# Contracting the gate broadcasts and logit turns of a two-layer PLE kernel over all 128 partitions

## Chip, cores and metric

The kernel runs on one core of one Trainium2 chip. The metric is the device time of one launch in microseconds (us). A core has TensorE (PE; its weight loads, PEld, are recorded apart), VectorE (DVE), ScalarE (ACT), GpSimd (POOL) and the queue engine SyncE (SP). Each engine works through its own instructions in order; semaphores tie them together.

## What is computed

For 1024 samples five table rows of 1024 numbers are gathered, and two layers of gated experts and a small tower run on them. A layer (T = 4 tasks, E = 10 experts, two of them shared) is:

```python
eo = relu(einsum('bed,edh->beh', xe, W) + b)
gates = softmax(einsum('btd,tdk->btk', x[:, :T, :], Gw) + Gb, axis=-1)
task_out = einsum('btk,btkh->bth', gates, sel_eo)      # k = 4: two own experts, two shared
gs = softmax(x[:, T, :] @ Gsw + Gsb, axis=-1)          # layer 0 only, over all 10 experts
shared_out = einsum('be,beh->bh', gs, eo)
```

The task outputs of layer 1, joined with 16 dense features, go through relu(4112 x 512), relu(512 x 256) and 256 x 1.

## The kernel before

The batch is worked in two halves of N = 512 samples. Activations lie transposed, features on the 128 partitions and samples on the 512 columns, so that everything the experts compute is a matmul with a 128 x 128 weight tile held in the array and 128 x 512 activations moving. Every fp32 product is made of three fp32r products (high x high, high x low, low x high) in the helper `three` (L296 to L298). One unit (`unit`, L300) is 8 x 3 such matmuls, the output of one 128-row strip of an expert, and a step is 16 units, two experts.

SP loads a raw weight tile for each unit, ACT rounds it (L498, w_hi), DVE subtracts (L797, w_lo), and PE multiplies. ACT takes each result out of PSUM with bias and relu (L502); DVE multiplies experts by gates and adds (L866, L872). The next step's activations are split by ACT (L513) and DVE (L804).

Gates are made alongside, within the first four units of each gated step (`gated_step`, L382). There are 18 gated steps: in each half one for the shared gates of layer 0, four for its tasks, and four for the tasks of layer 1. The order on PE is written out by hand through `between`, which puts instructions after the three matmuls of tile k of a unit:

- unit 0: `logits` (L331, L333), two matmuls per tile k, with a 128 x 66 gate-weight tile held in the array, into bank gps[0]. ACT copies the result into `logit_t` (L529), rows 0 to 7 or 0 to 19; row 32 holds ones and meets the bias row of `comb`.
- unit 1, after k = 3: `turn_logits` (L339, L351). Four fp32 matmuls with 33 rows: 33 x 128 of `logit_t` is held, `comb` (33 x 4 or 33 x 10) moves. This adds the high and low parts and the bias, and turns the logits so that samples lie on partitions. DVE and ACT make the softmax out of them (L818).
- unit 2, after k = 1: `turn_gates` (L362, L365), four matmuls that turn the gates back. ACT copies 12 rows into `gate_t`, which lies over the first 12 partitions of the gate-weight tile `gw` (L97, L538).
- unit 2, after k = 4, 6, 7, and unit 3, after k = 1, 3: `broadcast` (L369, L378). One matmul per gate, with 12 rows: a column of `pick`, repeated 128 times, is held, `gate_t` (12 x 512) moves, and the gate comes out on all 128 partitions. ACT copies it to `gate_b` (L521), which DVE reads. A shared step makes 2 broadcasts (both after k = 4), a task of layer 0 makes 6 (two after k = 4, the rest one by one), a task of layer 1 makes 4 (two after k = 4, one after k = 6, one in unit 3).

From the third broadcast on, PE waits before each (L376) until ACT has emptied the bank that it writes. Between layers the 16 dense features are multiplied with 16-row matmuls (L474). The input rows are gathered by POOL (L287) and turned by DVE (L939) during the first step of each half.

Before the loops DVE clears tiles and makes `pick` (L1023 to L1043), and ACT starts the loads of the constants, those of `comb` among them (L683 to L687).

Of the kernel before, what the change touches and what calls it, by code (L numbers as in the profile page):

```python
# [31 lines left out]
B, D, T, NE = 1024, 1024, 4, 10  # L32
P = 128
HALVES, N = 2, 512
# [7 lines left out]
NG = T  # L42
LOGIT_ROWS = 66
ONES_ROW = 32
# [19 lines left out]
def build(nc, ids, dense_t, tbl_0, tbl_1, tbl_2, tbl_3, tbl_4, w0, w1, w_top, w_dense, w_top2, w_top3,  # L64
          b0, b1, b_top1, b_top2, gs_w, g_w, g_b, comb_s, comb_t, gs_b, ident_in, out):
    f32, f32r, i32 = mybir.dt.float32, mybir.dt.float32r, mybir.dt.int32
    ALU, ACT, AX = mybir.AluOpType, mybir.ActivationFunctionType, mybir.AxisListType
# [3 lines left out]
    with ctx:  # L71
        def sb(name, shape, dt=f32):
            return ctx.enter_context(nc.sbuf_tensor(name, shape, dt))

        def bank(name):
            return ctx.enter_context(nc.psum_tensor(name, [P, N], f32))

        def sem(name):
            return ctx.enter_context(nc.semaphore(name))
# [12 lines left out]
        prod = sb("prod", [P, 2, N])  # L92
        gw_raw = sb("gw_raw", [P, KT * NE])
        gw = sb("gw", [P, KT, LOGIT_ROWS], f32r)
        logit_t = sb("logit_t", [ONES_ROW + 1, N])

        gate_t = gw[0:12, :, :].rearrange("p k n -> p (k n)")[:, 0:N]  # L97
        comb = sb("comb", [ONES_ROW + 1, NE + NG])
        comb_sh, comb_tk = comb[:, 0:NE], comb[:, NE:]
        lg = sb("lg", [P, NBT, NE])  # L100
        small = sb("small", [P, 2 * NBT + 2])
# [1 line left out]
        gsh = sb("gsh", [P, NBT, NE])  # L103
        g6 = sb("g6", [P, NBT, 6])
        g12 = sb("g12", [P, NBT, LOGIT_ROWS], f32r)
        pick = sb("pick", [12, 6], f32r)
        ident = prod[:, 0, 0:P]
        ident_r = sb("ident_r", [P, P], f32r)
        idx = sb("idx", [P, IDX], i32)
# [6 lines left out]
        gps = [bank(f"gps{i}") for i in range(2)]  # L116
# [35 lines left out]
        bc_done = sem("bc_done")  # L152
        gb_rdy = sem("gb_rdy")
        chain = sem("chain")
# [3 lines left out]
        y_done = sem("y_done")  # L158
        y_rdy = sem("y_rdy")
        pre_rdy = sem("pre_rdy")  # L160

        block = ctx.enter_context(nc.Block())

# [129 lines left out]
        def _(pe):  # L293
# [75 lines left out]
            def broadcast(Q, R, order, places):  # L369

                def emit(k):
                    for n in [i for i, at in enumerate(places) if at == k]:
                        if n == 0:
                            pe.wait_ge(gt_evac, Q + 1)
                        if n >= 2:
                            pe.wait_ge(gb_rdy, R + n - 1)  # L376
                        j = order[n]
                        nc.tensor.matmul(gps[1 - n % 2][:, :], pick[:, j:j + 1].broadcast_to([12, P]),  # L378
                                         gate_t, start=True, stop=True).then_inc(bc_done, 1)
                return emit  # L380

            def gated_step(U, E, S, Q, R, order, shared=0):  # L382
# [63 lines left out]
            for h in range(HALVES):  # L446
# [37 lines left out]
                n = T - 2  # L484
# [9 lines left out]
        def _(act):  # L494
# [187 lines left out]

            for dst, src in ((bias0, b0), (bias1, b1), (bias_t1, b_top1), (bias_t2, b_top2), (w3, w_top3)):  # L683
                act.dma_start(dst[:, :], src).then_inc(consts_in, 16)
            act.dma_start(comb_sh[0:ONES_ROW, :], comb_s).then_inc(consts_in, 16)
            act.dma_start(comb_sh[ONES_ROW:ONES_ROW + 1, :], gs_b).then_inc(consts_in, 16)
            act.dma_start(comb_tk[0:ONES_ROW, :], comb_t).then_inc(consts_in, 16)  # L687
# [89 lines left out]
        def _(dve):  # L777
            class Count:

                start, n = 0, 0  # L780

            links = Count()

            def link(ins):

                links.n += 1
                ins.then_inc(chain, 1)
                return links.start + links.n

            def after(value):  # L790
                dve.wait_ge(chain, value)
# [233 lines left out]
            nc.vector.memset(g6[:, :, :], 0.0).then_inc(chain, 1)  # L1025
            nc.vector.memset(warm[:, :], 0.0).then_inc(chain, 1)
            nc.vector.memset(g12[:, :, :].bitcast(f32), 0.0).then_inc(chain, 1)
            links.n = 5
            after(5)
            dve.wait_ge(idx_in, 16)  # L1030
            for q in range(Q4):
                part = idx[q * 32:(q + 1) * 32, NBT:]
# [6 lines left out]
            put_in_order(0)  # L1039
            dve.wait_ge(ident_rdy, 16)  # L1040

            after(link(nc.vector.tensor_tensor(pick[:, :], prod[0:12, 0, 0:6], prod[0:12, 0, 6:12], ALU.add)))
            nc.vector.tensor_copy(ident_r[:, :], ident).then_inc(pre_rdy, 1)  # L1043
            dve.wait_ge(pre_rdy, 1)
            put_in_order(2)
# [155 lines left out]
```

## Time and profile before

| | |
|---|---|
| median of 3 runs | 2163.16 us (2161.07 to 2168.05) |
| span of the profiled execution, first to last instruction | 2130.1 us |
| what lies around the span, by subtraction from the median | 33.1 us |
| PE busy | 98% |
| DVE busy | 64% |
| ACT busy | 36% |
| POOL busy | 7% |
| mean granted TensorE clock | 0.996 |

In the rows below a timeline row is: start, duration, engine, line, operation, output<-inputs, shape, count, and in brackets the idle time before it with what ended it. A matmul `12*128 12x512` has 12 rows and 128 columns held in the array, and 12 x 512 moving. Matmuls are pipelined, so their durations overlap; the distance from start to start says what one costs. A row with x8 stands for eight instructions in succession, and its second number reaches from the first's start to the last's end.

### The profile page before, as it was taken

The numbers are of one execution on the slowest core, as the hardware profiler recorded it, in microseconds if no ns is written. First come the engines' busy times: TensorE is split into PE (matmuls) and PEld (weight loads), VectorE is DVE, ScalarE is ACT, GpSimd is POOL, SyncE is SP. The second block draws the span as 40 slices with busy tenths as digits, with TensorE's granted clock in tenths as the row PEclk, the third lists the DMA queues.
The fourth block names the chain that finished last, engine by engine and source line by source line (L and its number), as shares of the span: only waits on it lengthen the run. The fifth ranks groups of instructions, "written<-read, shape, count | busy, mean of one in ns | idle before, by whom it ended". The sixth has DMA issues, their size and how long they took to land.

```text
span 2130.1 us, 27384 instructions
## 1 busy us (share of the span) xinstructions
PE 2096.8 (98%) x9148; PEld 1678.2 (79%) x9148; DVE 1361.7 (64%) x1521; ACT 774.0 (36%) x1068; POOL 151.4 (7%) x152
## 2 busy tenths in 40 slices
PE   7999999999999999999998999999999999999999
PEld 6878787778878787878786787877887787878787
DVE  4668787886256665646656687877853466556564
ACT  3243333333333333332433333334333333433333
POOL 5700000000000000000455000000000000000000
PEclk9999999999999999999999999999999999999999
DMA  6623223222233222223454222232332222323231
GB/s 193 189 88 98 80 89 89 89 89 89 81 91 97 87 94 87 89 89 99 137 162 148 81 95 80 88 90 87 90 98 81 89 89 89 99 79 97 82 97 40
DMA packets 62801, 208.08 MB, mean 98 GB/s; under 512 B 11668, under 2 KB 11988, under 8 KB 62742
## 3 DMA queue, kind: packets, MB, share of 16 engines
q1 hardware_dynamic: 54432, 186.30, 28.6%
q0 software_dynamic: 7488, 20.98, 3.1%
q8 instruction: 27, 0.44, 0.1%
q14 instruction: 32, 0.26, 0.0%
q10 hardware_dynamic: 822, 0.09, 0.0%
HBM read 207.34 MB, written 0.00 MB: 97 GB/s over the span
## 4 chain that ended last, share of the span: by engine, by line
PE 89%; POOL 6%; issue 2%; DVE 2%; ACT 1%; DMA 1%; POOLq 0%; ACTq 0%; DVEq 0%
PE main L296 26%; PE main L298 25%; PE main L297 25%; POOL eo_b L287 6%; PE top L296 3%; PE top L298 3%; PE top L297 3%; PE gps L331 2%; PE gps L333 2%; PE gps L378 1%; PE gps L351 1%; DVE act_lo L804 1%; DVE slots L939 0%; DMA eo_sh<-in_tbl,idx 0%; DVE w_lo L797 0%
## 5 line engine op out<-in xcount | busy, mean ns | idle before, releaser
L296 PE MATMUL main<-act_hi,w_hi 128*128 128x512 f32 x2568 | 1012.9, 394 | 13.9 <-DVE act_lo L804 8.4
L298 PE MATMUL main<-act_hi,w_lo 128*128 128x512 f32 x2568 | 1002.1, 390 | 0.0
L297 PE MATMUL main<-act_lo,w_hi 128*128 128x512 f32 x2568 | 1001.6, 390 | 0.0
L797 DVE TENSOR_TENSOR w_lo<-raw,w_hi 128x1024 fp32r<-128x1024 f32 (+1 forms) x360 | 439.5, 1221 | 675.2 <-ACT w_hi L498 674.6
L498 ACT ACTIVATE w_hi<-raw 128x1024 fp32r<-128x1024 f32 (+1 forms) x360 | 380.4, 1057 | 1064.7 <-PE main L298 959.5
L296 PEld LDWEIGHTS main<-act_hi,w_hi 128*128 128x128 f32 x2568 | 482.8, 188 | 143.0 <-issue 30.9
L298 PEld LDWEIGHTS main<-act_hi,w_lo 128*128 128x128 f32 x2568 | 482.9, 188 | 101.9
L297 PEld LDWEIGHTS main<-act_lo,w_hi 128*128 128x128 f32 x2568 | 483.2, 188 | 97.5
L872 DVE TENSOR_TENSOR slots<-slots,prod 128x1024 f32<-128x1024 f32 (+1 forms) x200 | 244.7, 1223 | 5.9
L287 POOL DMA_INDIRECT eo_b<-in_tbl,idx x144 | 147.3, 1023 | 1001.2 <-DVE slots L872 915.9
L866 DVE TENSOR_TENSOR prod<-eo_sh,gate_b 128x1024 f32<-128x1024 f32 x136 | 165.6, 1218 | 1.0
L804 DVE TENSOR_TENSOR act_lo<-slots,act_hi 128x512 fp32r<-128x512 f32 x216 | 132.6, 685 | 4.1 <-ACT act_hi L631 2.5
L513 ACT ACTIVATE act_hi<-slots 128x512 fp32r (+1 forms) x208 | 119.1, 624 | 15.2 <-DVE slots L939 9.3
L296 PE MATMUL top<-act_hi,w_hi 128*128 128x512 f32 x264 | 103.3, 391 | 4.5 <-DVE act_lo L1010 4.5
L298 PE MATMUL top<-act_hi,w_lo 128*128 128x512 f32 x264 | 103.4, 392 | 0.0
L297 PE MATMUL top<-act_lo,w_hi 128*128 128x512 f32 x264 | 103.4, 392 | 0.0
L502 ACT ACTIVATE eo_b<-main,bias 128x512 f32<-128x512 f32 x128 | 85.8, 671 | 3.0 <-DVE slots L872 1.7
L502 ACT ACTIVATE slots<-main,bias 128x512 f32 (+1 forms) x128 | 85.5, 668 | 0.0
L872 DVE TENSOR_TENSOR slots<-slots,eo_b 128x1024 f32 (+1 forms) x64 | 78.3, 1223 | 2.5
L866 DVE TENSOR_TENSOR slots<-slots,gate_b 128x1024 f32 (+1 forms) x64 | 78.0, 1218 | 0.0
L866 DVE TENSOR_TENSOR eo_b<-eo_b,gate_b 128x1024 f32<-128x1024 f32 x64 | 78.0, 1218 | 0.0
L939 DVE STREAM_TRANSPOSE slots<-eo_b 128x256 f32<-128x256 f32 x144 | 51.0, 412 | 36.4 <-DMA eo_b<-in_tbl,idx 36.4
(80 smaller groups left out, 722.3 us busy)
## 6 DMA issues: line engine op xcount, KB each, us to landing
raw<-in_w SPq DMA_DIRECT2D x320, 512.0 KB, 3.6
raw<-in_w_top SPq DMA_DIRECT2D x32, 512.0 KB, 3.6
eo_b<-in_tbl,idx POOLq DMA_INDIRECT x144, 2.9
raw<-in_w_top SPq DMA_DIRECT2D x4, 256.0 KB, 2.6
gw_raw<-in_g_w SPq DMA_DIRECT2D x16, 16.0 KB
comb<-in_g_b SPq DMA_DIRECT2D x16, 0.0 KB
raw<-in_dense_t SPq DMA_DIRECT2D x4, 32.0 KB, 1.8
bias<-in_b ACTq DMA_DIRECT2D x2, 40.0 KB
```

The lines of the kernel that those rows point to most:

```text
L287: pool.indirect_dma_start(stage(g)[:, s, :], None, tables[t].rearrange("v (q n) -> (v q) n", q=Q4), bass.IndirectOffsetOnAxis(ap=idx[:, c: ...
L296: nc.tensor.matmul(dst, lhs_hi, rhs_hi, start=start, stop=False)
L297: nc.tensor.matmul(dst, lhs_hi, rhs_lo, start=False, stop=False)
L298: return nc.tensor.matmul(dst, lhs_lo, rhs_hi, start=False, stop=stop)
L498: nc.scalar.activation(w_hi[0:parts, slot, 0:cols], raw[0:parts, rawslot, 0:cols], ACT.Copy)\
L502: nc.scalar.activation(dst, src, ACT.Relu, bias=bias).then_inc(evac_done, 1)
L513: nc.scalar.activation(act_hi[:, bass.ds(k, 1), :], slots[:, bass.ds(chunk + k, 1), :], ACT.Copy).then_inc(act_hi_rdy, 1)
L797: nc.vector.tensor_tensor(w_lo[0:parts, slot, 0:cols], raw[0:parts, rawslot, 0:cols], w_hi[0:parts, slot, 0:cols], ALU.subtract).then_inc( ...
L804: nc.vector.tensor_tensor(act_lo[:, bass.ds(k, 1), :], slots[:, bass.ds(chunk + k, 1), :], act_hi[:, bass.ds(k, 1), :], ALU.subtract).then ...
L866: seen[name] = (chain, link(nc.vector.tensor_tensor(dst, src, gate(j), ALU.mult)))
L872: ins = nc.vector.tensor_tensor(dst, dst, x, ALU.add)
L939: ins = nc.vector.transpose(slots[:, t * KT:(t + 1) * KT, at:at + 32], stage(g)[:, s, :])
```

## The change

`logit_t`, `comb` and `pick` get 128 rows instead of 33, 33 and 12. `comb` and `pick` are cleared first, so that their further rows are zeros. Broadcasts and logit turns contract over all 128 rows. The further rows of the moving or held operand are the gate weights in `gw` and the ones in `logit_t`, and each of them meets a zero. DVE gets two more memsets ahead of the loops, and ACT a wait for that of `comb` ahead of its loads.

```diff
-        logit_t = sb("logit_t", [ONES_ROW + 1, N])
-
-        gate_t = gw[0:12, :, :].rearrange("p k n -> p (k n)")[:, 0:N]
-        comb = sb("comb", [ONES_ROW + 1, NE + NG])
+        logit_t = sb("logit_t", [P, N])
+
+        gate_rows = gw[:, :, :].rearrange("p k n -> p (k n)")[:, 0:N]
+        gate_t = gate_rows[0:12, :]
+        comb = sb("comb", [P, NE + NG])
...
-        pick = sb("pick", [12, 6], f32r)
+        pick = sb("pick", [P, 6], f32r)
...
+        comb_clear = sem("comb_clear")
...
-                        nc.tensor.matmul(gps[1 - n % 2][:, :], pick[:, j:j + 1].broadcast_to([12, P]),
-                                         gate_t, start=True, stop=True).then_inc(bc_done, 1)
+                        nc.tensor.matmul(gps[1 - n % 2][:, :], pick[:, j:j + 1].broadcast_to([P, P]),
+                                         gate_rows, start=True, stop=True).then_inc(bc_done, 1)
...
+            act.wait_ge(comb_clear, 1)
             act.dma_start(comb_sh[0:ONES_ROW, :], comb_s).then_inc(consts_in, 16)
...
-            links.n = 5
-            after(5)
+            nc.vector.memset(pick[:, :].bitcast(f32), 0.0).then_inc(chain, 1)
+            nc.vector.memset(comb[:, :], 0.0).then_inc(comb_clear, 1)
+            links.n = 6
+            after(6)
...
-            after(link(nc.vector.tensor_tensor(pick[:, :], prod[0:12, 0, 0:6], prod[0:12, 0, 6:12], ALU.add)))
+            after(link(nc.vector.tensor_tensor(pick[0:12, :], prod[0:12, 0, 0:6], prod[0:12, 0, 6:12], ALU.add)))
```

The call of `turn_logits` is unchanged in the text; since its two tiles are taller, its matmuls contract over 128 rows too.

## Rows read from the trace of the kernel before

**Rows 1.** Page, busy time, share of the span and instructions.
```profile
PE 2096.8 (98%) x9148; PEld 1678.2 (79%) x9148; DVE 1361.7 (64%) x1521; ACT 774.0 (36%) x1068; POOL 151.4 (7%) x152
```
**Rows 2.** Who waited for whom: us in total, times, longest.
```profile
PE main L296 <- DVE act_lo L804: 8.4, 5, 3.5
```
**Rows 3.** Groups by line and shape: busy us, mean ns, idle us before.
```profile
L378 PE MATMUL gps<-gw,pick 12*128 12x512 f32 x84 | 36.7, 470 | 0.0
```
**Rows 4.** Waits of PE's loads for L378: us in total, times, longest.
```profile
PEld gps L378 <- issue: 21.0, 58, 0.4
...
PEld gps L378 <- ACT gate_b L521: 2.9, 8, 0.4
```
**Rows 5.** Timeline, PE, around a single broadcast.
```profile
138.63 0.40 PE L298 MATMUL main<-act_hi,w_lo 128*128 128x512 f32 x1
138.96 0.49 PE L378 MATMUL gps<-gw,pick 12*128 12x512 f32 x1
139.37 0.50 PE L296 MATMUL main<-act_hi,w_hi 128*128 128x512 f32 x1
139.71 0.39 PE L297 MATMUL main<-act_lo,w_hi 128*128 128x512 f32 x1
```
**Rows 6.** Timeline, PE and ACT, around a pair of broadcasts.
```profile
136.38 0.40 PE L298 MATMUL main<-act_hi,w_lo 128*128 128x512 f32 x1
136.71 0.73 PE L378 MATMUL gps<-gw,pick 12*128 12x512 f32 x2
137.24 1.09 ACT L521 ACTIVATE gate_b<-gps 128x512 f32<-128x512 f32 x2 [1.88 <-PE gps L378]
137.70 0.40 PE L297 MATMUL main<-act_lo,w_hi 128*128 128x512 f32 x1
```
**Rows 7.** Timeline, PE and its loads, around a logit turn.
```profile
30.25 0.39 PE L298 MATMUL main<-act_hi,w_lo 128*128 128x512 f32 x1
30.56 0.96 PEld L351 LDWEIGHTS gps<-comb,logit_t 33*128 33x128 f32 x8 [0.35 <-issue]
31.55 0.19 PEld L296 LDWEIGHTS main<-act_hi,w_hi 128*128 128x128 f32 x1
31.89 0.40 PE L297 MATMUL main<-act_lo,w_hi 128*128 128x512 f32 x1
```
**Rows 8.** Timeline, PE and its loads, around a gate turn.
```profile
35.56 0.39 PE L298 MATMUL main<-act_hi,w_lo 128*128 128x512 f32 x1
35.56 0.48 PEld L365 LDWEIGHTS gps<-ident_r,g 128*66 128x66 f32 x4
36.31 0.39 PE L297 MATMUL main<-act_lo,w_hi 128*128 128x512 f32 x1
```
**Rows 9.** Timeline, PE, into the 16-row dense matmuls.
```profile
588.47 0.39 PE L298 MATMUL main<-act_hi,w_lo 128*128 128x512 f32 x1
588.79 0.49 PE L296 MATMUL top<-w_hi 16*128 16x512 f32 x1
589.13 0.39 PE L297 MATMUL top<-w_lo,w_hi 16*128 16x512 f32 x1
589.36 0.39 PE L298 MATMUL top<-w_hi,w_lo 16*128 16x512 f32 x1
```
**Rows 10.** Stretches: busy us (count) of PE, PEld, DVE, ACT, POOL; granted clock; DMA.
```profile
129.04:224.86 95.82, 95.82 (x420) 76.03 (x419) 75.58 (x77) 35.19 (x49) 0.00 (x0) 1.00 0.28 88
```
**Rows 11.** The same columns, two stretches of equal length at either clock.
```profile
118.57:122.00 3.43, 3.43 (x16) 2.48 (x15) 3.33 (x5) 0.00 (x0) 0.00 (x0) 1.00 0.05 2
...
593.03:596.44 3.41, 3.41 (x9) 2.50 (x9) 1.23 (x1) 1.06 (x1) 0.00 (x0) 0.50 0.76 256
```
**Rows 12.** Timeline, the last fp32 matmuls, 128 rows.
```profile
2126.06 1.88 PE L429 MATMUL gps<-eo_b,tower_c 128*1 128x512 f32 x4 [0.19 <-ACT eo_b L656]
```
**Rows 13.** Timeline, DVE and ACT ahead of the loops.
```profile
2.94 1.00 DVE L1033 TENSOR_SCALAR idx<-idx 32x144 int32<-32x144 int32 x4 [0.66 <-DMA idx<-in_ids]
3.13 0.45 ACTq L685 DMA_DIRECT2D comb<-in_comb_s  x1
```

## The prediction

> **What bounds the kernel now.** I read the busy shares first: PE is busy for 98% of the span, DVE for 64% [rows 1]. Then the waits, because overlapping matmuls make PE's busy share too kind: all the waits of L296 for the lower halves of activations come to 8.4 us, in five places [rows 2]. They lie where one stage ends. Within a stage PE sets the pace. One task of layer 0, from logit turn to logit turn, takes 95.82 us, in which DVE is busy for 75.58 and ACT for 35.19 [rows 10], and each w_hi and w_lo waits for PE to finish a unit. So what matters is the distance between PE's starts. That distance is 0.23 us, from 589.13 to the record behind it [rows 9] between two matmuls with 512 columns moving at the same height; in the long stretch at the full clock, 16 full-height matmuls start within 3.43 us, 15 distances of some 0.23 [rows 11].
>
> Around a broadcast the rhythm breaks. From the L298 ahead of it to the L297 behind it are three distances: 0.33 to L378, 0.41 to L296, 0.34 to L297, 1.08 us in all where three regular ones are 0.69 [rows 5]. The duration of L378, 470 ns in the mean [rows 3], hides this; only the starts show it. Around a pair the four distances make 1.32 us against 0.92 [rows 6].
>
> **Is it the height?** Three rows bear on it. The gate turn, full height with only 66 columns, also into bank gps and also behind a semaphore, takes 0.75 us from L298 to the second matmul behind it, four small matmuls included; its first load starts together with the L298 before it [rows 8]. The loads of L378 and L351 don't: they start 0.31 to 0.33 us after it [rows 5, 7]. And the dense matmuls, 16 rows high, with no gate, no repeated column and another bank, show the same pattern: 0.32 on the way in, 0.34 at the first, then 0.23 between two of the same height [rows 9]. 
>
> **The change, part by part.**
>
> Single broadcasts. There are 84 broadcasts [rows 3], and PE's loads for them stand behind 58 + 8 = 66 gaps [rows 4]. The code makes one pair in each of the 18 gated steps, so 84 - 36 = 48 are single, and 48 + 18 = 66 agrees. With 128 rows nothing changes height, and I take three regular distances: 1.08 - 0.69 = 0.39 us each, 48 x 0.39 = 18.7 us.
>
> Pairs. 1.32 - 0.92 = 0.40 us each, 18 x 0.40 = 7.2 us.
>
> Is a regular distance right for a repeated column of `pick`? No full-height row with one exists. The pair holds the nearest one: after the first broadcast the second follows so closely that the pair costs only 0.24 us more than a single (1.32 - 1.08), with the same repeated column. The upper bound of the cost is that the whole irregularity stays, a gain of nothing; I take the regular distance.
>
> Logit turns. Each is four fp32 matmuls that are recorded as eight loads and eight matmuls. The eight loads reach over 0.96 us; less the last one's own 0.19 that is 0.77 for seven distances, 0.11 each, with 4 or 10 columns moving, so the loads set the pace [rows 7]. From L298 to L297 it is 31.89 - 30.25 = 1.64 us. At full height I build it after the gate turn: first load beside the L298, first matmul 0.23 after it, seven load distances to the last, 0.77, one more load for L296, 0.11, and 0.23 from the load of L297 to its matmul. The load of L296 starts with the last matmul, at 1.00, that of L297 at 1.11, its matmul at 1.34. Gain 1.64 - 1.34 = 0.30, and 18 x 0.30 = 5.4 us. Bounds: nothing at all if tall fp32 loads can't be hidden, 0.40 x 18 = 7.2 if it behaves like a pair.
>
> The sum is 18.7 + 7.2 + 5.4 = 31.3 us.
>
> Ahead of the loops. `logit_t` is cleared over 128 partitions instead of 33, with the same 512 elements in each, and two tiny memsets join. DVE is idle for 0.66 us behind its memsets until the indices arrive [rows 13], which covers them; without cover they would cost some 0.2 us, an estimate. ACT's wait for `comb` stands ahead of three loads, the first issued at 3.13 us, and DVE is through with its old memsets 0.66 us before 2.94, at 2.28 [rows 13]. Queued behind it on ACT are those loads and the first w_hi; the wait should be over before it is reached. I cost all of it at zero.
>
> **Does the gain arrive?** Within a stage nothing else is near: after the change a task of layer 0 takes 95.82 - 4 x 0.39 - 0.40 - 0.30 = 93.6 us, DVE still 75.6 busy, or 81%. At the ends of stages PE waits for DVE to hand over activations, but DVE's work there is itself released by PE's last units, so both move together. The savings in the first step of each half (0.70 us each) could be eaten by the gathering of inputs, whose last set PE waits for; that is 1.4 us at most, and I leave it in. What is late next is what was late before.
>
> **The clock.** After some stalls between stages the granted clock falls to its lower level, 1.2 GHz (0.50) instead of 2.4: in equal stretches PE then starts 9 matmuls instead of 16 [rows 11]. Seven at 0.23 us is 1.6 us for such a stretch. The trace has five of them, all behind stalls at the joints of stages, none in a gated step's broadcasts, where the clock is 1.00 [rows 10]. When PE arrives earlier at these joints it can get one more or fewer. I forecast no change and allow three of them either way, 4.8 us.
>
> **Against the times.** The profiled span is 2130.1 us, which becomes 2130.1 - 31.3 = 2098.8. The 33.1 us around it stay, so 2131.9, and since 33.1 was made with the median this is 2163.2 - 31.3. I say 2132.
>
> **The rivals.**
>
> (A) A new wait in place of the gap. The third broadcast needs ACT's copy of the first (same bank), the fourth that of the second. ACT begins copying 0.53 us after the pair's first start and has both copied by 1.62 [rows 6]. The third broadcast, after tile k = 6, comes 8 x 0.23 = 1.84 after the pair, the fourth 0.92 later. So there is room of at least 0.2 us even against both copies. If the hand-over is longer than it looks, the 24 broadcasts after k = 6 and k = 7 keep their gap: 24 x 0.39 = 9.4 lost, 2141. The eight gaps put down to ACT's copy [rows 4] speak for it, but their length, 0.4 at most, is that of all the others.
>
> (B) Tall loads aren't hidden. Then the first load of a group and that of the L296 behind it each stand free, 0.11 apiece: a single costs 0.69 + 0.22 = 0.91, gain 0.17, 48 x 0.17 = 8.2; a pair has three free loads, 0.92 + 0.33 = 1.25, gain 0.07, 18 x 0.07 = 1.3; turns give nothing. 2163.2 - 9.5 = 2154. The gate turn's load, which starts with the L298 before it [rows 8], speaks against it. "TensorE: Matmul & The Clock Gate" in the Trainium skill, in its part on packing small matmuls, says that a load overlaps running matmuls only when it aims at other row groups; full-height loads never would. Here that rule and the row differ.
>
> (C) The height isn't the cause; a cost of the repeated column, the bank or the waits stays. Then nothing changes: 2163. The 16-row matmuls [rows 9] speak against it.
>
> (D) Slower: tall fp32 matmuls cost more. The only fp32 matmuls of this form with 128 rows are L429, four records in 1.88 us, one to the next some 0.43 (their 512 moving columns explain it) [rows 12]. If the turns' eight records took 0.43 each because they are tall, a turn would grow by 8 x (0.43 - 0.11) = 2.6 us, 18 x 2.6 = 46, and against the 31.3 the time would be 2178. It decides from (31.3 + 6.5) / 144 = 0.26 on top of 0.11, that is from 0.37 us a record, for a loss of 0.3%. Against it: 4 and 10 columns move, not 512.
>
> **Chances.** 0.3% is 6.5 us, about what a measurement of this kernel can tell from no change. Forecast 0.82; (A) 0.07; (B) 0.05; (C) 0.04; (D) 0.02. Faster is forecast, (A) and (B), 0.94; same is (C), 0.04; slower (D), 0.02. For the range: the gain without the turns is 25.9, with them like pairs 33.1, that is 2130 to 2137; the clock adds 4.8 on either side, which takes in (A) as well. So the range is 2130 - 5 = 2125 to 2137 + 5 = 2142.
>
> **What would show it.** Loads of L378 and L351 with 128 rows that start with the L298 before them; 0.69 from L298 to L297 around a single, 0.92 around a pair, 1.34 around a turn; a task of layer 0 in 93.6 us. The step on the turns is wrong if their eight matmuls are more than 0.11 apart. (A) would show as starts of L378 after k = 6 and 7 that stand later than those after k = 4. The gaps around the 16-row matmuls must stay. The total would be off if a stall at a joint grew by what the stage saved.

## The result

The changed kernel took 2136.99 us in the median of four runs (2134.03 to 2138.78); the kernel before took 2165.61 us beside it. The ratio is 0.9872, with a 95% interval of 0.9852 to 0.9891: 28 us less, 24 to 32. The forecast was 2132 us, with a range from 2125 to 2142.

The added lines shift the numbers: L298, L299, L300, L353, L367, L380 and L800 of the changed kernel are L296, L297, L298, L351, L365, L378 and L797 of before. Where a single broadcast stood behind a gap of 0.33 us [rows 5], the timeline of PE and its loads now has:

```profile
158.16 0.39 PE L300 MATMUL main<-act_hi,w_lo 128*128 128x512 f32 x1
158.16 0.19 PEld L380 LDWEIGHTS gps<-gw,pick 128*128 128x128 f32 x1
158.39 0.40 PE L380 MATMUL gps<-gw,pick 128*128 128x512 f32 x1
158.62 0.39 PE L298 MATMUL main<-act_hi,w_hi 128*128 128x512 f32 x1
158.85 0.40 PE L299 MATMUL main<-act_lo,w_hi 128*128 128x512 f32 x1
```

The load starts with the matmul before it, and the three distances are 0.23, 0.23 and 0.23, 0.69 together instead of 1.08. All 48 single broadcasts show 0.68 to 0.70. Around a pair, PE and ACT:

```profile
156.31 0.40 PE L300 MATMUL main<-act_hi,w_lo 128*128 128x512 f32 x1
156.54 0.63 PE L380 MATMUL gps<-gw,pick 128*128 128x512 f32 x2
156.98 1.09 ACT L523 ACTIVATE gate_b<-gps 128x512 f32<-128x512 f32 x2 [1.69 <-PE gps L380]
157.24 0.40 PE L299 MATMUL main<-act_lo,w_hi 128*128 128x512 f32 x1
```

That is 0.93 us instead of 1.32 [rows 6]; all 18 show 0.93 or 0.94. Around a logit turn, PE and its loads:

```profile
148.91 0.40 PE L300 MATMUL main<-act_hi,w_lo 128*128 128x512 f32 x1
148.92 1.09 PEld L353 LDWEIGHTS gps<-comb,logit_t 128*128 128x128 f32 x8
149.15 0.95 PE L353 MATMUL gps<-comb,logit_t 128*128 128x4 f32 x8
149.93 0.19 PEld L298 LDWEIGHTS main<-act_hi,w_hi 128*128 128x128 f32 x1
150.27 0.39 PE L299 MATMUL main<-act_lo,w_hi 128*128 128x512 f32 x1
```

From the L300 to the L299 it is 150.27 - 148.91 = 1.36 us, where before had 1.64 [rows 7]; all 18 show 1.36. One task of layer 0, from logit turn to logit turn, takes 93.56 us, where it took 95.82 [rows 10].

The page has these busy times and shares (compare [rows 1]):

```profile
PE 2082.1 (97%) x9148; PEld 1692.9 (79%) x9148; DVE 1361.8 (64%) x1523; ACT 773.5 (36%) x1068; POOL 152.7 (7%) x152
```

PE is busy for 14.7 us less. But its span is 2137.0 us, longer than the 2130.1 of the profile of before, though the kernel is 28 us faster; and the run's own time was 2138.78, only 1.8 us above its span. So the 33 us between the median of before and its profiled span can't lie around the span. To see where they lie I cut both executions at the first matmul of logit turns: up to the second turn (this holds the first step, with the gathering), to the tenth, to the eleventh (the second half's first step), and to the end. Columns are stretch, length, then busy us and count of PE, PEld, DVE, ACT and POOL, granted clock, DMA share and GB/s. Before:

```profile
0.00:129.04 129.04, 113.72 (x498) 91.74 (x498) 73.53 (x136) 44.52 (x62) 70.21 (x72) 0.99 0.55 173
129.04:1074.64 945.60, 941.28 (x4117) 754.26 (x4116) 615.59 (x647) 346.52 (x478) 23.97 (x24) 1.00 0.30 93
1074.64:1185.18 110.54, 103.30 (x444) 81.22 (x443) 66.14 (x117) 38.59 (x54) 57.26 (x56) 0.98 0.48 148
1185.18:2130.10 944.92, 938.53 (x4093) 751.00 (x4092) 606.40 (x624) 344.34 (x474) 0.00 (x0) 1.00 0.28 87
```

After:

```profile
0.00:149.15 149.15, 123.06 (x499) 97.37 (x500) 73.46 (x138) 44.78 (x62) 68.88 (x72) 0.91 0.49 150
149.15:1084.77 935.62, 929.62 (x4118) 759.40 (x4117) 615.45 (x647) 346.09 (x478) 24.00 (x24) 0.99 0.31 94
1084.77:1208.29 123.52, 107.20 (x444) 83.06 (x443) 66.41 (x117) 38.69 (x54) 59.79 (x56) 0.94 0.44 132
1208.29:2137.00 928.71, 922.24 (x4093) 753.09 (x4091) 606.48 (x624) 343.96 (x474) 0.00 (x0) 1.00 0.29 88
```

The second and fourth stretch lost 10.0 and 16.2 us. The first and the third, the steps with the gathering, are 20.1 and 13.0 us longer, and the granted clock there is 0.91 and 0.94 instead of 0.99 and 0.98. The waits of the changed kernel over the whole span (us in total, times, longest) hold four kinds of wait that the profile of before doesn't have at all:

```profile
ACT w_hi L500 <- remote: 59.0, 6, 13.9
...
DVE w_lo L800 <- issue: 40.2, 10, 7.6
...
ACT w_hi L500 <- issue: 29.3, 5, 13.6
...
PE main L298 <- issue: 6.2, 3, 3.4
```

"Remote" means that the view found no releaser it knows. The timeline inside the first step shows it on PE: within one unit, successive matmuls stand 1.17 and 1.40 us apart behind "issue" time, while POOL issues gathers:

```profile
118.11 0.39 PE L299 MATMUL main<-act_lo,w_hi 128*128 128x512 f32 x1
...
119.08 0.94 POOL L289 DMA_INDIRECT eo_b<-in_tbl,idx  x1 [0.30 <-issue]
119.28 0.40 PE L300 MATMUL main<-act_hi,w_lo 128*128 128x512 f32 x1 [0.78 <-issue]
...
120.02 0.48 PE L299 MATMUL main<-act_lo,w_hi 128*128 128x512 f32 x1
...
121.42 0.59 PE L300 MATMUL main<-act_hi,w_lo 128*128 128x512 f32 x1 [0.92 <-issue]
```

Either the change brought this, or the profile of before was taken where it doesn't happen. That became the main question of the experiments; the other was whether it is the height alone that makes the gaps.

### The profile page after: what moved, and what is told of

Read it like the earlier page. It is cut to its first block, busy times and chain, and to the rows that moved or that the text cites. A ratio compares the mean times of both kernels' runs of the same rounds, so it can differ in the third digit from the quotient of the medians.

```text
span 2137.0 us, 27386 instructions
## 1 busy us (share of the span) xinstructions
PE 2082.1 (97%) x9148; PEld 1692.9 (79%) x9148; DVE 1361.8 (64%) x1523; ACT 773.5 (36%) x1068; POOL 152.7 (7%) x152
## 3 DMA queue, kind: packets, MB, share of 16 engines
q1 hardware_dynamic: 54432, 186.30, 28.6%
## 4 chain that ended last, share of the span: by engine, by line
PE 92%; issue 3%; DVE 2%; another core or an unknown queue 1%; ACT 1%; DMA 1%; POOL 0%; DVEq 0%; ACTq 0%
PE main L298 26%; PE main L300 26%; PE main L299 26%; PE top L298 3%; PE top L300 3%; PE top L299 3%; PE gps L333 2%; PE gps L335 2%; PE gps L380 1%; PE gps L353 1%; DVE act_lo L807 1%; DVE w_lo L800 1%; ACT w_hi L500 0%; DVE slots L942 0%
## 5 line engine op out<-in xcount | busy, mean ns | idle before, releaser
L298 PE MATMUL main<-act_hi,w_hi 128*128 128x512 f32 x2568 | 1011.4, 394 | 32.2 <-DVE w_lo L800 12.9
L300 PE MATMUL main<-act_hi,w_lo 128*128 128x512 f32 x2568 | 1007.3, 392 | 4.8 <-issue 4.7
L299 PE MATMUL main<-act_lo,w_hi 128*128 128x512 f32 x2568 | 1006.5, 392 | 2.6 <-issue 2.5
L800 DVE TENSOR_TENSOR w_lo<-raw,w_hi 128x1024 fp32r<-128x1024 f32 (+1 forms) x360 | 439.3, 1220 | 676.7 <-ACT w_hi L500 635.8
L500 ACT ACTIVATE w_hi<-raw 128x1024 fp32r<-128x1024 f32 (+1 forms) x360 | 380.3, 1056 | 1094.7 <-PE main L300 902.2
L298 PEld LDWEIGHTS main<-act_hi,w_hi 128*128 128x128 f32 x2568 | 486.2, 189 | 150.8 <-issue 29.9
L300 PEld LDWEIGHTS main<-act_hi,w_lo 128*128 128x128 f32 x2568 | 485.7, 189 | 108.1 <-issue 5.2
L299 PEld LDWEIGHTS main<-act_lo,w_hi 128*128 128x128 f32 x2568 | 486.2, 189 | 104.9 <-issue 3.9
L298 PE MATMUL top<-act_hi,w_hi 128*128 128x512 f32 x264 | 102.9, 390 | 0.7 <-DVE act_lo L1013 0.7
L300 PE MATMUL top<-act_hi,w_lo 128*128 128x512 f32 x264 | 102.7, 389 | 0.0
L299 PE MATMUL top<-act_lo,w_hi 128*128 128x512 f32 x264 | 102.7, 389 | 0.0
```

What stands on the lines that cost most here:

```text
L298: nc.tensor.matmul(dst, lhs_hi, rhs_hi, start=start, stop=False)
L299: nc.tensor.matmul(dst, lhs_hi, rhs_lo, start=False, stop=False)
L300: return nc.tensor.matmul(dst, lhs_lo, rhs_hi, start=False, stop=stop)
L500: nc.scalar.activation(w_hi[0:parts, slot, 0:cols], raw[0:parts, rawslot, 0:cols], ACT.Copy)\
L800: nc.vector.tensor_tensor(w_lo[0:parts, slot, 0:cols], raw[0:parts, rawslot, 0:cols], w_hi[0:parts, slot, 0:cols], ALU.subtract).then_inc( ...
```

## The experiments

The runs were made on three different chips, up to four kernels on each, and which chip it was turned out to matter.

**First chip: before again, each part alone, and 64 rows.**

The kernel before, unchanged. 

> The kernel before, unchanged, timed against itself and profiled once more. The profile that the prediction was read from has a span of 2130.1 us, while the profile of the changed kernel has 2137.0 us, with the run's own time only 1.8 us more. Theory: that profiled execution of before was one in which the first step of each half (gathering) ran undisturbed, and the usual execution of before has some 30 us more inside its span, not around it. Then the new profile has a span of about 2160 us, a first half's first step (up to the second logit turn) of 112 to 120 us instead of 98.5, and the same 95.8 us for a task of layer 0. Rival (what the prediction said): the 33 us lie around the span; then the new profile's span is 2130 again. Either way the ratio is 1.000, within 0.003.

Its profiled span is 2155.4 us, with 142.86 us to the second turn and 116.87 from the tenth to the eleventh. From the first turn to the second it is 112.05 us, at the lower end of what was expected, and a task of layer 0 takes 95.81. 12 runs had a median of 2163.85, those of the kernel before beside it 2163.16, ratio 1.0003 (0.999 to 1.0016). Its waits have the same kinds as those of the changed kernel above ("ACT w_hi L498 <- remote" 41.6 us, "DVE w_lo L797 <- issue" 43.7 us). So the stalls are in before too, inside its span: the theory holds, and the sentence of the prediction on the 33.1 us is wrong.

Only the broadcasts over 128 rows:

```diff
-                                              logit_t[:, bt * P:(bt + 1) * P], adder, start=True, stop=True)
+                                              logit_t[0:33, bt * P:(bt + 1) * P], adder[0:33, :], start=True, stop=True)
```

> Only the broadcasts contract over 128 rows, the logit turns over 33 as before. Theory: 48 x 0.39 + 18 x 0.39 = 25.7 us less, ratio 0.988; a single broadcast 0.69 us from L298-line matmul to the second behind it, a pair 0.92, a turn still 1.63. Rival (tall and short matmuls cost only at the first change of height in a step, so that doing one part alone brings less than its share): well under 20 us less.

Ratio 0.9895 (0.9876 to 0.9914): 22.7 us less, 18.6 to 26.8. By the starts, the 48 singles were 0.68 to 0.70, the 18 pairs 0.93 or 0.94 and the 18 turns 1.63 or 1.64 us. The gaps went at full price; the total came 3 us short of it, within the interval. The rival, that one part alone brings less than its share because the first change of height in a step is what costs, is out by these distances.

Only the turns over 128 rows:

```diff
-                        nc.tensor.matmul(gps[1 - n % 2][:, :], pick[:, j:j + 1].broadcast_to([P, P]),
-                                         gate_rows, start=True, stop=True).then_inc(bc_done, 1)
+                        nc.tensor.matmul(gps[1 - n % 2][:, :], pick[0:12, j:j + 1].broadcast_to([12, P]),
+                                         gate_rows[0:12, :], start=True, stop=True).then_inc(bc_done, 1)
```

> Only the logit turns contract over 128 rows, the broadcasts over 12 as before. Theory: 18 x 0.27 = 4.9 us less, ratio 0.9977; a turn 1.36 us, a single broadcast still 1.08, a pair 1.32. Rival (turns gain as pairs would, 0.40 each): 7.2 us, ratio 0.9967, and a turn of 1.24 us.

Ratio 0.9988 (0.9977 to 0.9998): 2.6 us less, 0.4 to 5.0. Single 1.08, pair 1.32, turn 1.36. The theory's 4.9 lies at the end of the interval; the rival's 7.2 is outside it, and its 1.24 us for a turn was not seen. The two parts alone give 25.3 together, both of them about 28.

Broadcasts over 64 rows:

```diff
-pick[:, j:j + 1].broadcast_to([P, P]), gate_rows,
+pick[0:64, j:j + 1].broadcast_to([64, P]), gate_rows[0:64, :],
```

> The changed kernel with broadcasts over 64 rows instead of 128 (turns tall). It tells whether the gap needs full height or only more rows than 12. Theory (any matmul whose rows don't reach the full height stands in another division of the array): the gaps are those of before, 1.08 and 1.32 us, whatever the number of rows. Rival (the gap shrinks with the rows that are missing): about half of 0.39, that is 0.87 us around a single.

One run, 2161.38 us, the level of before on this chip with the turns' small gain; a single run shows no more, and the distances decide. PE's timeline around a single broadcast:

```profile
157.30 0.39 PE L300 MATMUL main<-act_hi,w_lo 128*128 128x512 f32 x1
157.62 0.49 PE L380 MATMUL gps<-gw,pick 64*128 64x512 f32 x1
158.04 0.50 PE L298 MATMUL main<-act_hi,w_hi 128*128 128x512 f32 x1
158.38 0.40 PE L299 MATMUL main<-act_lo,w_hi 128*128 128x512 f32 x1
```

0.32, 0.42 and 0.34, or 1.08 in all (1.07 to 1.10 in the 48), and 1.32 around each pair: the gap is what it was with 12 rows. Five times as many rows take nothing off it.

**Second chip: the changed kernel again, 96 rows, and both kernels without indirect gathers.**

The changed kernel, unchanged. 

> The changed kernel, unchanged, timed and profiled again, to narrow the ratio. The regular part is settled by the traces: 18.7 + 6.9 + 4.9 = 30.5 us by rows (0.39 a single, 0.386 a pair, 0.272 a turn). Theory: all of it arrives but what is saved inside the first step of each half, 2 x (0.39 + 0.27) = 1.3 us, where PE waits for other things afterwards: 29 us less than before, ratio 0.9865. Rival: the first steps lose more time in the changed kernel than in before (the first two profiles say 149.2 + 123.5 against 142.9 + 116.9 us up to the second turn and from the tenth to the eleventh), so that some 5 to 13 us of the gain are given back: ratio 0.989 or above, and again over 270 us for these two stretches.

On this chip the kernel before took 2135.76 us, 27 us less than on the first chip, and the changed one 2106.22. The ratio is 0.9866 (0.9851 to 0.9881), 28.6 us. The same four stretches, and they can be set beside those of before above, since neither has the stalls (chips or executions without them are called quiet from here on):

```profile
0.00:130.02 130.02, 114.23 (x498) 92.88 (x499) 73.48 (x138) 44.38 (x62) 69.38 (x72) 0.97 0.55 172
130.02:1062.29 932.27, 927.96 (x4117) 759.05 (x4116) 615.28 (x647) 346.18 (x478) 23.97 (x24) 1.00 0.31 94
1062.29:1173.41 111.12, 103.96 (x444) 82.66 (x443) 66.49 (x117) 38.61 (x54) 58.53 (x56) 0.97 0.48 147
1173.41:2102.10 928.69, 922.20 (x4093) 753.62 (x4091) 606.55 (x624) 344.00 (x474) 0.00 (x0) 1.00 0.28 88
```

The rival's 270 us for the first and third stretch came out as 241.1; the theory's 0.9865 was met. Its reason, that the saving inside the first step of each half doesn't arrive, isn't borne out by the two runs with plain loads below, which show that saving.

Broadcasts over 96 rows: as with 64, with 96 in its place. 

> The changed kernel with broadcasts over 96 rows (turns tall). With 64 rows the gaps were wholly there, 1.09 us around a single. Theory (the array is divided into halves or quarters of its rows, and 96 rows fit neither, so they stand in the undivided array): no gap, 0.69 us around a single, 0.93 around a pair, as with 128. Rival (only all 128 rows avoid it): 1.08 and 1.32 us.

```profile
138.78 0.39 PE L300 MATMUL main<-act_hi,w_lo 128*128 128x512 f32 x1
139.01 0.40 PE L380 MATMUL gps<-gw,pick 96*128 96x512 f32 x1
139.24 0.40 PE L298 MATMUL main<-act_hi,w_hi 128*128 128x512 f32 x1
139.48 0.40 PE L299 MATMUL main<-act_lo,w_hi 128*128 128x512 f32 x1
```

Distances of 0.23, 0.23 and 0.24, and one run of 2105.44 us. A pair took 0.94. So 96 rows are as good as 128, and 64 as bad as 12. Nothing between 64 and 96 was tried.

The gathers replaced by plain loads of the same size, in the changed kernel. The gathering by index is left out: every load reads the first 128 rows of its table's view, so the addresses no longer scatter either.

```diff
-                        pool.indirect_dma_start(
-                            stage(g)[:, s, :], None, tables[t].rearrange("v (q n) -> (v q) n", q=Q4),
-                            bass.IndirectOffsetOnAxis(ap=idx[:, c:c + 1], axis=0)).then_inc(x_in[g % 2], 16)
+                        pool.dma_start(
+                            stage(g)[:, s, :],
+                            tables[t].rearrange("v (q n) -> (v q) n", q=Q4)[0:P, :]).then_inc(x_in[g % 2], 16)
```

> The changed kernel with the 144 indirect gathers of the first steps replaced by plain loads of the same size from fixed rows (the gathering by index is left out, so its inputs are other rows). It asks where the first steps of each half lose their time. Theory: PE, ACT and DVE are starved there by the gathers (their waits are put down to issue and to an unknown releaser, 36.6 + 14.6 us on ACT up to 130 us), and with plain loads the stretch up to the second turn falls from 149 to some 130 us, that from the tenth to the eleventh turn from 123 to some 110, about 30 us in all. Rival: the stalls come from the amount of data that is moved, or from the weight loads alone, and stay.

2086.84 us, 19.4 below the changed kernel on the same chip. Since this chip had no stalls to take away, the 30 us of the expectation could not be seen here; 124.63 and 101.41 us for the two stretches are 5.4 and 9.7 less than with gathers.

The same in the kernel before. 

> The kernel before with the same replacement of the gathers by plain loads (the gathering by index is left out). Together with the changed kernel in the same state it gives the gain with the disturbance of the first steps taken out, if it is taken out. Theory: slower than the changed kernel with plain loads by 30.5 us, and by 1.6 us more or less for each half-clock stretch that differs. Rival (the first steps eat a share of the gain even when undisturbed): 29 us or less.

2116.12 us, so 29.3 us separate the two. In its profile the stretches are 125.39, 942.85, 102.12 and 943.41 us, in that of the changed kernel 124.63, 929.49, 101.41 and 931.54. The small savings in the first steps are there now, 0.76 and 0.71 where the rows give 0.66; in the long stretches it is 13.4 and 11.9, with 3.4 and 6.8 us more at the lower clock. The theory's 30.5 less a clock term holds, the rival doesn't, as far as the first steps are concerned.

**Third chip: both kernels once more, and plain loads where the stalls are.**

Before. 

> The kernel before once more, unchanged, as the companion of the next two. So far its median was 2163 us on one chip and 2136 us on another, and the whole difference lies in the first step of each half (142.9 + 116.9 us against 129.0 + 110.5). Theory (a property of the chip, not of the kernel): this call shows one of the two levels again, and before and changed stand at the same one. Rival (a matter of the single execution): a value in between, with profiles of either kind in one call.

Changed. 

> The changed kernel a third time. Theory: 28 to 31 us less than before on the same chip, ratio 0.986 to 0.987, whichever level the chip shows. A second question is the clock: the changed kernel's quiet profile had 23.9 us at the lower level where that of before had 17.0. If that is chance, this pair may show it the other way round; if the change brings it, the changed kernel has the longer time at the lower level again.

Changed with plain loads. 

> The changed kernel with the gathers replaced by plain loads from fixed rows (gathering by index left out), a second time. If the chip is a disturbed one (before at some 2163 us): theory that indirect gathers are what is disturbed expects 2087 us as on the quiet chip; the rival, that all of the first step's traffic is slower there, expects some 2100 us or more. On a quiet chip it repeats 2087 us and tells nothing new.

Before took 2160.85 and 2161.64 us in the medians of its two labels, so this was a chip with the stalls. The theory that before and changed show one of two levels, and nothing in between, holds. The changed kernel took 2139.46, ratio 0.9896 (0.987 to 0.9923), 22.5 us less, 17 to 28. That is under the expected 28 to 31; the expectation's 0.986 lies just outside the interval, 0.987 on its edge. On its second question, the clock, the answer is the one against chance: 61.4 us at the lower level in the profile of the changed kernel, 44.4 in that of before. With plain loads it took 2087.47, the same as on the quiet chip. So what is disturbed on some chips is the step with indirect gathers: they cost 2139.46 - 2087.47 = 52 us here and 19 there. The first and third stretch, before with gathers on this chip:

```profile
0.00:146.86 146.86, 122.09 (x499) 95.62 (x499) 73.62 (x136) 44.90 (x62) 69.09 (x72) 0.93 0.49 152
...
1099.22:1220.08 120.86, 104.49 (x444) 81.03 (x443) 65.75 (x117) 38.62 (x54) 57.09 (x56) 0.96 0.45 135
```

and the changed kernel with plain loads on this chip:

```profile
0.00:124.70 124.70, 111.58 (x499) 90.72 (x500) 73.47 (x138) 44.48 (x62) 38.16 (x72) 0.99 0.57 180
...
1052.62:1153.99 101.37, 100.19 (x443) 80.41 (x442) 66.27 (x117) 38.64 (x54) 29.69 (x56) 1.00 0.52 161
```

POOL is busy for 38 us instead of 69 in the first stretch, DMA moves more per second, and PE gets on.

## Why the prediction was right, and where it wasn't

**Height and the broadcasts: right.** The step "a change of height is what costs, on the way in and on the way out" rested on the 16-row matmuls [rows 9] and on the gate turn [rows 8]. 48 x 0.39 and 18 x 0.39 (0.40 in the forecast) make 25.7 us. With 96 rows no gap and with 64 rows the whole of it, in kernels that differ in nothing else, the height is shown to be the cause. Rival (C), another cause than the height, fell with the first timeline. The gaps around the 16-row matmuls stayed, as they should (PE in the changed kernel's second profile, compare [rows 9]):

```profile
580.53 0.39 PE L300 MATMUL main<-act_hi,w_lo 128*128 128x512 f32 x1
580.85 0.49 PE L298 MATMUL top<-w_hi 16*128 16x512 f32 x1
581.19 0.39 PE L299 MATMUL top<-w_lo,w_hi 16*128 16x512 f32 x1
```

The Trainium skill's sentence on draining when the tiling mode changes ("TensorEngine Tiling (Array Packing)", Key Properties) and its list of modes (128, 64 or 32 rows, same page, Available Configurations) agree with 64 against 96 rows: the gap is there at 12, 16 and 64 rows and gone at 96.

**Loads: right.** Rival (B) said that tall loads can't be hidden; the load of L380 starts with the L300 before it. The sentence of the Trainium skill's page "TensorE: Matmul & The Clock Gate" that the prediction drew on (the part on packing small matmuls) has this the other way round for loads at the same rows, and the timeline decides against it. The same part also says that a load into the background weight buffer is pulled ahead, and with that the timeline agrees. In the changed kernel's first profile 8372 of the 8590 loads with 128 rows and 128 columns that follow a matmul of that shape start within 0.02 us of its start.

**Turns: a term slightly too large.** Forecast 0.30 each, measured 1.64 - 1.36 = 0.28, the same in the mean of the 18, so 5.0 us instead of 5.4. The construction after the gate turn was right in its parts: the last load of the turn is followed by that of L298 at 149.93, 1.02 after the L300 where 1.00 was put down, and the L299 stands at 1.36 where 1.34 was. (D), dear tall fp32 matmuls, is out: the eight stand 0.11 apart.

**No new wait (A): right.** The broadcasts after k = 6 and 7 show the same 0.69. ACT copies the pair from 156.98 to 158.07, and the next broadcast starts at 158.39.

**Ahead of the loops: right.** The two memsets are done at 2.33, the indices' work starts at 3.02 instead of 2.94, and ACT issues the load of `comb` at 3.14 instead of 3.13 [rows 13]:

```profile
2.26 0.07 DVE L1032 MEMSET comb<- 128x14 f32 x1
...
3.02 1.00 DVE L1038 TENSOR_SCALAR idx<-idx 32x144 int32<-32x144 int32 x4 [0.69 <-DMA idx<-in_ids]
3.14 0.44 ACTq L688 DMA_DIRECT2D comb<-in_comb_s  x1
```

**"The 33.1 us around it stay": wrong.** What lies around the span is 1.8 us. The profile of before came from an execution without the stalls in the first steps, the timed runs from ones with them. The failing step is the subtraction of a span from a median that belong to different conditions. It did no harm to the time, since the gain was set against the median, and the gain is of one size in all three comparisons: 28 us, 28.6 and 22.5, with overlapping intervals. That the time itself fell into the range of 2125 to 2142 is in part luck of the chip: on the second chip the same two kernels gave 2135.76 and 2106.22, outside it, with the same gain. Of the 5 us between 2132 and 2136.99, 2.4 are that before took 2165.61 beside the changed kernel, not 2163.2. It did harm to what the sum leaves out: some 30 us of stalls, as large as the gain, were in no row.

**The clock: the size was right, the guess of no change wasn't.** By the clock record of the trace the profile of before has 17.1 us at the lower level, the changed kernel without stalls (second chip) 23.9. In the four stretches it is 3.4, 3.4, 3.4 and 6.8 us for before, 6.8, 6.8, 6.8 and 3.4 for the changed kernel. At 1.6 us for each 3.4, the prediction's price, the stretches should differ by -0.66 + 1.6, -14.7 + 1.6, -0.66 + 1.6 and -14.7 - 1.6, that is 0.9, -13.1, 0.9 and -16.3; measured are 1.0, -13.3, 0.6 and -16.2. The parts make 27.5 of the 28.0 us by which the two spans differ. (14.7 is the share of a long stretch: four tasks with four singles and a pair, four with two and a pair, eight turns.)

One pair of profiles could be chance, but all the others point the same way. In the profiles the changed kernel has 54.6 us at the lower level against 41.0 (the first profile, and before on the first chip), 61.4 against 44.4 (third chip), and with plain loads 20.5 against 10.2. The mean granted clock of all executions (three digits for each) gives the same: 0.9940 in 4 executions against 0.9950 in 9 on the second chip, 0.9873 in 4 against 0.9902 in 23 on the third, 0.9966 in 5 against 0.9975 in 4 with plain loads, and on the first chip 0.9882 with the broadcasts alone (6) and 0.9883 with the turns alone (12) against 0.9897 (35). Since the lower level is half, twice what the mean clock lacks to 1, times the span, is the time at it, and at 1.6 us for each 3.4 these differences cost, as an estimate, 1.9, 5.7, 1.7, 2.8 and 2.9 us. Taken off what the distances between starts give (48 x 0.39, 18 x 0.38 and 18 x 0.28, 30.7 us for the whole, 25.7 for the broadcasts, 5.0 for the turns), they leave 28.8, 25.0, 29.0, 22.9 and 2.1, where 28.6, 22.5 (17 to 28), 29.3, 22.7 and 2.6 were measured. By this estimate the step "I forecast no change" is the one that made the forecast gain of 31.3 us too large. Why the changed kernel spends more time at the lower level isn't shown; on the chips with stalls the lower clock may also stand for longer stalls and not be their price.

**Does the gain arrive?** Where the first steps run undisturbed, yes, less the clock. Where they don't, 24 to 32 us and 17 to 28 arrived. The profiles have 272.7 and 272.0 us in the first and third stretch for the changed kernel and 259.7 and 267.7 for before, with 41 and 44 us at the lower clock against 27 and 31. That looks as if some 4 us or more of the gain were given back there. But the kernels in between, on the first chip, have 268.4 (broadcasts alone), 269.7 (turns alone) and 267.8 (64 rows), each a single execution, so whether the change does that or the choice of executions isn't settled: the intervals of all three comparisons overlap at 0.987 to 0.988.

What the stalls are can be read one step further. ACT's long waits "remote" are waits for PE: each w_hi (L500) needs a slot that PE frees with the last matmul of a unit, two units back. In the profile of before, w_hi usually starts 0.43 us after the start of that matmul. In the stall of the changed kernel that matmul starts at 114.26 and its w_hi at 126.36, 12.10 us later:

```profile
114.26 0.39 PE L300 MATMUL main<-act_hi,w_lo 128*128 128x512 f32 x1
...
126.36 1.06 ACT L500 ACTIVATE w_hi<-raw 128x1024 fp32r<-128x1024 f32 x1 [13.90 <-remote]
```

The record of that semaphore has no rise between these two until 126.34, 0.02 us ahead of ACT, and the other late w_hi of that step (53.55, 73.61, 93.69 and 110.83) stand 0.02 or 0.03 us behind a recorded rise as well. DVE's long waits "issue" for w_lo end as ACT's w_hi ends (w_hi from 73.61 to 74.67, w_lo at 74.77), so DVE only follows. So this doesn't look like engines that are each starved on their own. As the record has it, PE's signal reaches ACT up to 12 us late, ACT and DVE follow, and PE then lacks weights (11.1 us of waits for w_lo in the first stretch, none in the profile of before). Beside that PE's own matmuls stand apart, mostly by 0.7 us or a multiple of it.

Part of the labels is a gap in the record. In all seven profiles with stalls semaphore records are missing (of the four times 1440 landings of weight loads, the changed kernel's first profile has 1410, 1370, 1374 and 1407), in all six quiet ones none is. That leaves a rival that no run tests: the recording itself may be part of what is held up, or hold up the engines; and where a rise is missing, a late signal and an ACT that was held up itself look alike. Nor is it settled why it happens only on some chips. That the gathers are needed for it is shown; whether by their handling on POOL or by their scattered rows is not, since the plain loads changed both.

## What to carry to other kernels

Read TensorE by the distances between starts. In this kernel a matmul of 512 columns that contracts over 12 or 64 rows and stands among full-height ones costs some 0.39 us beyond its own slot, and another one right behind it at the same height costs nothing more. Pad such a matmul with zeros to 96 or 128 rows (fewer than 96 wasn't tried), or put all of them together. And before a profile's span is set against a median, compare it with the time of that same run: in every run here for which both are on record they were 1.8 us apart. If the span lies much further from the median, the profile shows another condition than the runs, and what it lacks may be as large as what is being changed.

## What the hardware showed that was not expected

The kernel before took 2136 us on one chip and 2161 to 2166 us in the other three comparisons, with most of the difference in the two steps with indirect gathers (20 to 28 us by the profiles of before; another 5 to 7 us in the stretch between them); with plain loads of the same size the changed kernel took 2087 us on either kind of chip. On the chips with stalls, single matmuls of those steps stood 0.7 to 2.8 us apart behind "issue" time, many of them by 0.7, 1.4, 2.1 or 2.8, ACT's w_hi started up to 12 us after the matmul of PE that it waits for instead of 0.43, and the granted clock in the first 149 us of the changed kernel fell to 0.91. And the height of a matmul counts in coarse steps: with 12, 16, 33 and 64 rows the first load starts 0.31 to 0.33 us after the matmul before it, with 96 rows it starts together with it, as with 128.
